# VectorE's program of three relational graph layers written out pair by pair, with its job registers loaded once a pair

## The reference

```python
edge_w = edge_attr @ nn_w.T + nn_b
msg = jax.nn.relu(x[src] * edge_w)
out = x @ root + bias
for r in range(N_REL):
    mask = edge_type == r
    m = jnp.where(mask[:, None], msg, 0.0)
    s = jax.ops.segment_sum(m, dst, num_segments=n)
    cnt = jax.ops.segment_sum(mask.astype(x.dtype), dst, num_segments=n)
    mean = s / jnp.maximum(cnt, 1.0)[:, None]
    out = out + mean @ W[r]
```

## Time and profile before

| | us |
|---|---|
| median of three runs | 4999.56 |
| the profiled execution, first to last instruction (its span) | 4117.9 |
| median less span | 881.7 |
| first relational layer, first gather to end of last add | 573.6 |
| second | 581.6 |
| third | 581.4 |

### The profile page before, as it was taken

One profiled execution on the slowest core, in us unless ns is written; L12 is line 12 of the kernel. 1 busy time (PEld: TensorE's weight loads), 2 busy tenths in 40 slices (PEclk: granted clock), 3 DMA queues, 4 the chain that ended last, 5 costly groups with the idle time before them and its releaser, 6 DMA issues.

```text
span 4117.9 us, 112272 instructions
## 1 busy us (share of the span) xinstructions
PE 3104.7 (75%) x28301; PEld 2331.3 (57%) x28301; DVE 2876.4 (70%) x10466; ACT 1533.8 (37%) x4045; POOL 2706.7 (66%) x2886
## 2 busy tenths in 40 slices
PE   6886027777776987777648888897888888888887
PEld 4443015555554565555436666676666667666666
DVE  9998026777776677777667777766777766777777
ACT  1000006777764267777623333212333321333320
POOL 5777747777774377777647777636777745777760
PEclk8777558999998999999969999899999989999988
DMA  3222157888884578888834444314443323444430
GB/s 77 55 57 48 27 162 218 237 237 236 237 230 84 162 228 238 237 237 236 200 108 124 123 120 120 108 58 125 122 120 115 114 73 90 122 119 117 116 105 32
DMA packets 386267, 574.01 MB, mean 139 GB/s; under 512 B 134783, under 2 KB 272433, under 8 KB 386163
## 3 DMA queue, kind: packets, MB, share of 16 engines
q0 software_dynamic: 155264, 442.19, 37.8%
q1 hardware_dynamic: 176106, 123.76, 10.1%
q10 hardware_dynamic: 54794, 6.81, 1.1%
HBM read 531.37 MB, written 41.08 MB: 139 GB/s over the span
## 4 chain that ended last, share of the span: by engine, by line
PE 19%; issue 19%; DVE 16%; DVEq 10%; DMA 10%; POOL 7%; ACT 2%; ACTq 1%; POOLq 0%; SPq 0%
DMA ht<-kv_rows,gidx 6%; PE bank L1210 6%; DVE region L1873 6%; DVEq L728 4%; PE bank L1049 3%; POOL ht L584 3%; PE bank L1197 3%; DVE rings L1854 3%; DMA gring<-kv_rows,gidx 2%; DVE rings L1860 2%; POOL gring L618 2%; PE bank L1124 2%; POOL gring L584 2%; PE bank L1145 2%; PE bank L1157 1%
## 5 line engine op out<-in xcount | busy, mean ns | idle before, releaser
L618 POOL DMA_INDIRECT gring<-h_rows,gidx x1248 | 1201.1, 962 | 464.3 <-issue 317.2
L1210 PE MATMUL bank<-rings 128*128 128x96 f32 x6168 | 914.8, 297 | 247.2 <-DVE region L1873 245.3
L1210 PEld LDWEIGHTS bank<-rings 128*128 128x128 f32 x6168 | 811.0, 205 | 444.8 <-DVE region L1873 406.8
L1281 ACT ACTIVATE rings<-rings 128x512 f32<-128x512 f32 x771 | 485.6, 630 | 1366.2 <-DVE rings L1854 1313.0
L1854 DVE TENSOR_TENSOR rings<-bank,gring 128x256 f32<-128x256 f32 x1542 | 582.4, 420 | 390.1 <-PE bank L1210 195.2
L584 POOL DMA_INDIRECT gring<-kv_rows,gidx x512 | 485.7, 949 | 245.9 <-issue 133.4
L1873 DVE TENSOR_TENSOR region<-region,bank 128x192 f32 x1542 | 540.0, 350 | 131.8 <-PE bank L1210 14.7
L584 POOL DMA_INDIRECT ht<-kv_rows,gidx x512 | 486.2, 950 | 173.7 <-issue 118.4
L1322 ACT ACTIVATE ht<-ht,ntop 128x129 f32<-128x129 f32 x1024 | 413.8, 404 | 287.0 <-DVE ntop L1788 278.4
L1197 PE MATMUL bank<-nnwt,rings 64*128 64x256 f32 x3084 | 491.0, 442 | 39.1 <-DMA rings<-edge_attr_T 39.1
L559 POOL DMA_INDIRECT edge_records<-rings x416 | 408.3, 981 | 151.3 <-issue 148.5
(11 more groups left out here) (257 smaller groups left out, 4095.4 us busy)
## 6 DMA issues: line engine op xcount, KB each, us to landing
rings<-node_in_window_T SPq DMA_DIRECT2D x256, 128.0 KB
rings<-edge_attr_T SPq DMA_DIRECT2D x1548, 16.0 KB
gring<-h_rows,gidx POOLq DMA_INDIRECT x1248
kv_rows<-rows SPq DMA_DIRECT2D x50, 258.0 KB, 2.5
rows<-h_rows SPq DMA_DIRECT2D x75, 128.0 KB
gring<-kv_rows,gidx POOLq DMA_INDIRECT x512
ht<-kv_rows,gidx POOLq DMA_INDIRECT x512
region<-edge_records SPq DMA_DIRECT2D x13, 576.0 KB, 7.0
```

Of the source, the lines that this page charges most:

```text
L618: g.indirect_dma_start(out=gring_r[:, 2 * u + k, :], out_offset=None, in_=h_d[l], in_offset=bass.IndirectOffsetOnAxis(ap=gidx_r[:, half, 2 ...
L1210: ins = pe.matmul(b[:, (2 * k + c) * SEG:(2 * k + c + 1) * SEG], prod[:, slot % RL, (2 * k + c) * P:(2 * k + c + 1) * P], one, start=True, ...
L1281: act.activation(prod[:, slot % RL, :], prod[:, slot % RL, :], ACT.Relu).then_inc(s_msg, 1)
```

## The change

DVE's loop is gone. `related` is written out for all 257 pairs of each layer, so every semaphore value, `prod` slot, bank and column of `seg_j` is a constant. The order inside a pair is new: product, add, product, add, then the one-hot masks every second pair, then the register load for the next pair. The wait for the `prod` slot and that for the `oh` buffer fall away, since the wait in front of the first add covers them.

The table of job numbers is laid out as records of five numbers a pair (`PREC`) instead of twenty for four pairs; the load reads one record, and the wait value for `s_land` is masked and raised by one or two register operations. On POOL the number of the pair to wait for is masked too (`& FREEMASK`), which turns one register instruction of each step into a move and two operations.

```diff
             def load(p, base):
+                regs = sets[p % RL]
+                eng.reg_load(regs, job_t[:, p * PREC:(p + 1) * PREC])
+                eng.reg_alu(counts[p % RL], regs[4], LANDMASK, ALU.bitwise_and)
+                if base:
+                    eng.reg_add(counts[p % RL], counts[p % RL], base)
...
-                        freed = g.snap(free_regs[u], min_val=1, max_val=RPAIRS)
+                        freed = g.snap(free_regs[u], min_val=1, max_val=RPAIRS) & FREEMASK
...
+            load_job(0, l * GPAIRS)
+            for p in range(RPAIRS + LAG_RACC):
+                new, old = p < RPAIRS, p >= LAG_RACC
+                if new:
+                    v.wait_ge(s_land, landed(p))
+                    if p % 2 == 0:
+                        v.wait_ge(s_ew, l * RQUADS + p // 2 + 1)
+                    product(p, 0)
+                if old:
+                    v.wait_ge(s_sp, at + p - LAG_RACC + 1)
+                    if l and p == LAG_RACC:
+                        v.wait_ge(s_clr, 2 + l * NT)
+                    add_sums(p - LAG_RACC, 0)
+                if new:
+                    product(p, 1).then_inc(s_prod, 1)
+                if old:
+                    add_sums(p - LAG_RACC, 1)
+                if new and p % 2 == 0:
+                    v.tensor_tensor(oh[:, p // 2 % 2, :, :],
+                                    seg_j[:, 2 * p:2 * p + Q].unsqueeze(2).to_broadcast([P, Q, SEG]),
+                                    iota_seg[:, :].unsqueeze(1).to_broadcast([P, Q, SEG]), ALU.is_equal).then_inc(s_oh, 1)
+                if p + 1 < RPAIRS:
+                    load_job(p + 1, l * GPAIRS)
```

More of the change, by code:

```diff
@@ L57 @@
 HREC = HALF + HALF + HALF // 2
+PREC = 5
 GT = CT // TU
@@ L60 @@
 LAND = 2
+FREEMASK, LANDMASK = 511, 255
 PITCH = 512
@@ L387, in build @@
         tab = rings[0:1, after_stage:after_stage + TAB + 2 * JOBC].bitcast(I32)
-        tab_job = tab[:, 0:HALVES * HREC].rearrange("o (h i) -> o h i", i=HREC)
+        tab_job = tab[:, 0:HALVES * HREC].rearrange("o (p i) -> o p i", i=PREC)
         tab_free = tab[:, HALVES * HREC:TAB]
@@ L723, in job_registers, with load, window, place @@
         def job_registers(eng):
-            sets = [[eng.alloc_register(f"job{h}_{i}") for i in range(HREC)] for h in range(2)]
-            def load(half, pair):
-                eng.reg_load(sets[half], job_t[:, bass.ds(pair * (HREC // (U // 2)), HREC)])
-            def window(slot, k):
-                return eng.snap(sets[slot // (U // 2)][2 * (slot % (U // 2)) + k], min_val=0, max_val=NW)
-            def place(slot, k):
-                return eng.snap(sets[slot // (U // 2)][HALF + 2 * (slot % (U // 2)) + k], min_val=0, max_val=TU - 1)
-            def landed(slot):
-                return eng.snap(sets[slot // (U // 2)][2 * HALF + slot % (U // 2)], min_val=1, max_val=GPAIRS)
+            sets = [[eng.alloc_register(f"job{h}_{i}") for i in range(PREC)] for h in range(RL)]
+            counts = [eng.alloc_register(f"landed{h}") for h in range(RL)]
+            def load(p, base):
+                regs = sets[p % RL]
[3 more added lines that the diff above has]
+                    eng.reg_add(counts[p % RL], counts[p % RL], base)
+            def window(p, k):
+                return eng.snap(sets[p % RL][k], min_val=0, max_val=NW)
+            def place(p, k):
+                return eng.snap(sets[p % RL][2 + k], min_val=0, max_val=TU - 1)
+            def landed(p):
+                return counts[p % RL]
             return load, window, place, landed
@@ L1652, in tables_of_tiles @@
             step(v.tensor_scalar(tab_free, tab_free, 1, None, ALU.logical_shift_right))
-            step(v.tensor_copy(tab_job[:, :, 0:HALF], tab_win.rearrange("o (h i) -> o h i", i=HALF)))
+            step(v.tensor_copy(tab_job[:, :, 0:2], tab_win.rearrange("o (p k) -> o p k", k=2)))
             after()
-            tiles = tab_tile.rearrange("o (h i) -> o h i", i=HALF)
-            step(v.tensor_scalar(tab_job[:, :, HALF:2 * HALF], tiles, TU - 1, None, ALU.bitwise_and))
-            step(v.tensor_scalar(tab_job[:, :, 2 * HALF:HREC], tiles[:, :, 1::2], 1, None, ALU.logical_shift_right))
+            tiles = tab_tile.rearrange("o (p k) -> o p k", k=2)
+            step(v.tensor_scalar(tab_job[:, :, 2:4], tiles, TU - 1, None, ALU.bitwise_and))
+            step(v.tensor_scalar(tab_job[:, :, 4], tiles[:, :, 1], 1, None, ALU.logical_shift_right))
             after()
-            tell("tab", v.tensor_scalar(tab_job[:, :, 2 * HALF:HREC], tab_job[:, :, 2 * HALF:HREC], 1, None, ALU.add))
+            tell("tab", v.tensor_scalar(tab_job[:, :, 4], tab_job[:, :, 4], 1, None, ALU.add))
         def edges_of_tiles(v, step, after, tell):
@@ L1876, in related, with product, add_sums @@
-            run_steps(v, REXTRA + LAG_RACC, step, RTRIPS)
+            load_job, window, place, landed = job_regs
+            def product(p, k):
+                row = gring_r[:, bass.ds(place(p, k), 1), :].rearrange("p o f -> p (o f)")
+                weights = bank[p // 2 % 2 * 2 + k][:, p % 2 * D:(p % 2 + 1) * D]
+                return v.tensor_tensor(prod[:, p % RL, k * D:(k + 1) * D], weights, row, ALU.mult)
+            def add_sums(p, k):
+                wait_freed(v, s_racc, 2 * (at + p) + k)
+                o = racc[:, :, bass.ds(window(p, k) * W, W)]
+                sums = bank[RL + p % RS][:, 2 * k * SEG:2 * (k + 1) * SEG]
+                v.tensor_tensor(o, o, sums.rearrange("p (s d) -> p s d", d=W), ALU.add).then_inc(s_racc, 1)
```

33 lines of the change are left out of this document (removed).

## The result

| | us |
|---|---|
| kernel before, median of four runs | 4999.51 (4994.37 to 5001.6) |
| changed kernel, median of four runs | 5077.55 (5065.44 to 5081.13) |
| ratio | 1.016, 95% interval 1.0144 to 1.0176 |
| profiled execution of the changed kernel, its time and its span | 5081.13, 5079.3 |

The change makes the kernel 78 us slower, where 108 us less were forecast. And the time of the profiled execution lies 1.8 us from its span: nothing of size lies around the span.

What follows compares the result with a forecast made beforehand. POOL's gathers were to become the pace: 529 + 7 = 536 us, then 536 - 1 + 8 = 543 a layer. Savings of 31 + 39 + 38 = 108 us from 4999.6 gave 4892 us, range 4870 to 4964.

Steps and rivals of the forecast that it cites:

- The dense part, the attention layers and the time around the span stay: Outside the changed layers: nothing changes, including 881.7 us taken to lie around the profiled span of 4117.9 us.
- Five take 0.41 by my estimate: DVE's new register load in each pair: five numbers last 0.41 us, from 0.063 a number and 0.095 on top.
- the first sign of being wrong that I had named: DVE's register load L733: the prediction is wrong if a load lasts over 0.7 us.
- The upper bound that I named: Price of DVE's new load: bounded above by ACT's strided load of four numbers, 0.89 us.
- the register load does not shrink with its numbers: Rival at L733, before each first product: five numbers cost 1.35 us like twenty, time about 5480 us; chance 0.06.
- Behind masks the load should be hidden: DVE in pairs with masks: the sequencer runs ahead and hides the load, so a pair takes about 1.9 us.
- POOL as the pace: POOL's gathers set each layer's pace: 536 us of gathers, 543 us a layer; chance 0.68.
- the tail: End of a layer, last gather's start to last add's end: falls from 21.0 us to 8 us.
- I leave it a fifth of its 32 us of blocks, 7: POOL's time blocked by slots not free in a layer: falls from 32 us to 7.
- they cost nothing as long as gathers are queued: POOL's two more register operations a step: free under queued gathers, otherwise up to 28 us a layer.
- I give nothing more: Register instructions of DVE's removed loop: already inside the counted gaps of 116 us a layer, so no further saving.

Runs made afterwards that it cites:

- e3_quad_timed: Changed kernel with one aligned register load of 20 numbers for four pairs instead of one a pair: 4080.9 us, ratio 0.9912, kernel before at 4117.3.
- e11: Same kernel as e3_quad_timed, run again where the kernel before takes about 5000 us: 5077.0 us, ratio 1.0065.
- e5: Changed kernel with both products first, then masks and both adds, the load of every pair behind them: 4570.5 us, ratio 1.1106, kernel before at 4117.3.
- the first job's single runs: Kernel before with its loaded counts masked, 5027.7 us; changed kernel with one 20-number load for four pairs, 5021.1; kernel before 5000.4.
- e13: e5 with the load of every pair moved between the two adds: 5085.6 us, ratio 1.0098, where the kernel before takes about 5000.
- e8: Changed kernel with aligned records of four numbers, slot and count made by three more register operations: 4107.1 us beside 4123.5, single run.
- e6: The changed kernel, unchanged, timed where the kernel before takes 4123.5 us: 4190.3 us, ratio 1.0166.
- e9: Kernel of e3_quad_timed with its table shifted by one word, so no load begins at a multiple of 16 bytes: 5195.5 us, single run.

## Why the prediction was wrong

The step that failed is the price of the new register load, and a second one failed beside it, the base.

*The base.* "The dense part, the attention layers and the time around the span stay", with 881.7 us around the span. But the profile's own execution must have taken about 4120 us: in every execution here that has both, time and span lie under 2 us apart. This did not turn the sign of the change itself (its ratio is 1.016 at both levels). It set every number in microseconds against the wrong time, and it hid that the timed runs are paced otherwise than the profile: the adds' wait for PE's sums in the second layer is 83 us in the one and 11 in the other. A kernel with cheap loads gains at the profile's level and loses at that of the timed runs (e3_quad_timed, e11).

*The load.* At the low level its price turned the sign: with quad loads (0.9912) or four aligned words (4107.1 beside 4123.5) the rest of the change gains. At the high level, where the forecast was tested, it made most of the loss, 57 of 78 us; the ratio falls from 1.016 to 1.0065 with quad loads, and doesn't go below 1. "Five take 0.41 by my estimate" was worked out from two rows whose records both begin at a multiple of 16 bytes and are a multiple of 16 bytes long. What the runs show is 0.34 for four such numbers, 0.59 for five that begin there, 0.60 for eight, 1.35 for twenty; and 1.18 for five that begin elsewhere, 4.49 for twenty. On DVE all of it fits 0.25 us a started group of four plus 0.1 where the record is aligned, and 0.22 to 0.24 a number where it isn't. The mean of the 771 loads is 1.04, 0.63 over my price, and the first sign of being wrong that I had named, a load over 0.7, is there. The upper bound that I named, ACT's 0.89 for four, shows the same price of 0.22 a number. ACT reads every second word of the very records that DVE loads whole in 0.598, so there it isn't the start that costs; whether it is the stride or the engine, no run tells. But the row did show that a price of this size exists.

The Trainium skill ("Runtime: NRT & Kernel Launch", "Instruction fetch mechanics") gives about 200 ns a register even in bulk. The page speaks there of register loads from HBM, and those here come from SBUF. DVE's loads that are not aligned come near it in the traces, with 0.22 to 0.24 us; the aligned ones are 1.7 times (five words) to 3 times (twenty) shorter than by that rule. I had set it aside on the evidence of aligned loads alone.

The rival *the register load does not shrink with its numbers*, with a chance of 0.06, had the right place, L733 in front of each first product, and the measured load lies on the side of its 0.70 us where it said the change loses. Its 1.35 us was too high, and its account, that five cost what twenty do, is not what the runs show. At its 1.0 us it gave 2.53 us a pair; the layer at the low level shows 608.2/257 = 2.37, since the load is hidden longer than I had thought.

*Hiding.* "Behind masks the load should be hidden": it starts even before the last add, and a pair with masks takes no longer than one without, 2.40 and 2.43 us. This step was right as far as it went: the masks' 0.46 us are hidden. In the old order, where the load starts behind both adds, the same loads made the change cost 11% at the low level (e5) instead of 1.7.

*POOL as the pace* was right where the load is cheap, at the low level. With quad loads DVE waits 357.5 us for gathers, the tail falls from 21 to 11 us (8 forecast), and the layers last 561, 569 and 565 us against 543 forecast. The step "I leave it a fifth of its 32 us of blocks, 7" was mis-sized: some 22 to 30 stay. So even with cheap loads the gain at the low level is 36 us (quad loads) or 16 (four words a pair, one run), not 108. So with the load as cheap as I priced it, the forecast would still have been three times too large or more.

*The register instructions.* For POOL's masks the prediction has "they cost nothing as long as gathers are queued", and the trace bears it out for most of them. For DVE's masks it has no term at all; in the old loop the masks cost 86 us at the low level. Of the loop's own register instructions it says "I give nothing more"; writing the loop out won 108 us. The two nearly cancel, which is luck.

The parts at the low level, in us: masks +86, written out -108, alternating -14, loads pair by pair +103 (each kernel set against the kernel before of its own job). They add up to the measured 67 by construction, since each is the step from one kernel to the next, and they hold only in this order: taken before the alternation the pair loads cost 475, and the alternation then gives some 380 back. At the high level the first job's single runs give masks +27, written out and alternating together -7, pair loads +57.

Left open is what the high level is, and with it why the change loses some 0.65% there even with quad loads. The traces of that level show instructions that start late with nothing to wait for, on DVE, POOL, ACT and PE, in untouched code too, and a granted clock of about 0.82 where the kernel before has 0.89 at the low level. The instructions of DVE and POOL themselves last the same at both (the rows of adds and gathers above), so they don't run slower, they start later. No run could switch the level on or off.

## What to carry to other kernels

Before adding a profile's parts up against a timed median, compare its span with the times. Here the two lie under 2 us apart in one execution, so a gap of hundreds of microseconds means other conditions, and not time around the span. DVE's register load is priced here by where its record begins, so pad records to 16 bytes before splitting them, or load several at once. And look at what the instruction ahead of a load waits for: in e5 a load behind an add that waits lies mostly bare, and in e13 the same load one place earlier is nearly hidden.

## What the runs showed of the hardware that I had not expected

- A register load of DVE from SBUF: 0.34 us for 4 words (e8), 0.59 for 5 (e6), 0.60 for 8 and 1.35 for 20 where the record begins at a multiple of 16 bytes; 1.18 for 5 (e6) and 4.49 for 20 (e9) where it doesn't.
- DVE starts such a load while one operation still runs and two more are queued (e6, e13), but not before an instruction ahead of it has done its wait (e5). In a pair with masks DVE then idles 0.65 us in e6 and 0.31 in e13, against 1.2 in e5.
- The same program on one core takes 4117 to 4124 us in some jobs and 4998 to 5052 in others, with the granted clock at about 0.89 and 0.82, on one and the same chip too; and a change may gain 0.9% at one level and lose 0.65% at the other.
